# An edge loop on one core: a register load and score sums moved behind an aggregation, exponents ahead of one-hot rows, rectification one step earlier into six places

## The reference

```python
h_src = h[src]; h_dst = h[dst]                       # h: 6250 x 8 heads x 32
alpha = einsum(h_src, a_src) + einsum(h_dst, a_dst)
enc = relu(edge_attr @ edge_W.T + edge_b)            # 100000 x 8 x 32
alpha = alpha + sum(enc * h_dst, axis=-1)
alpha = where(alpha >= 0, alpha, 0.2 * alpha)
ex = exp(alpha - segment_max(alpha, dst)[dst])
out = segment_sum(h_src * ex / segment_sum(ex, dst)[dst], dst)
```

## Time and profile before

| | |
|---|---|
| median of three runs | 2097.55 us |
| the profiled execution | 2095.04 us, span 2093.2 us |
| mean granted TensorE clock | 0.968 |
| `edges`, first encoding to last sum | 102 to 1169 us |
| PE busy | 1919.5 us (92%) |
| DVE busy | 1517.0 us (72%) |
| ACT busy | 1290.6 us (62%) |
| POOL busy | 1206.5 us (58%) |

### The profile page before, as it was taken

One profiled execution on the slowest core, in us unless ns is written; L12 is line 12 of the kernel. 1 busy time (PEld: TensorE's weight loads), 2 busy tenths in 40 slices (PEclk: granted clock), 3 DMA queues, 4 the chain that ended last, 5 costly groups with the idle time before them and its releaser, 6 DMA issues. The chain is left out here.

```text
span 2093.2 us, 45236 instructions
## 1 busy us (share of the span) xinstructions
PE 1919.5 (92%) x12492; PEld 1499.5 (72%) x12492; DVE 1517.0 (72%) x3421; ACT 1290.6 (62%) x3667; POOL 1206.5 (58%) x1137
## 2 busy tenths in 40 slices
PE   7679999999999999999999486899999999999997
PEld 5446666666666666666666245899999999999996
DVE  8769899999999999999999878444444444444442
ACT  4458888888898888888898475233333333333332
POOL 3377777777777776766664000455555555555553
PEclk9879999999999999999999788999999999999998
DMA  9555555555555555555553895222222222222221
GB/s 253 163 153 151 150 157 153 155 153 158 155 155 150 154 151 147 146 144 145 145 141 91 282 331 80 54 36 39 39 36 36 38 40 37 36 36 39 39 37 23
DMA packets 161230, 242.12 MB, mean 116 GB/s; under 512 B 36895, under 2 KB 115519, under 8 KB 160866
## 3 DMA queue, kind: packets, MB, share of 16 engines
q0 software_dynamic: 61920, 139.45, 28.2%
q1 hardware_dynamic: 90362, 92.12, 15.0%
q10 hardware_dynamic: 8712, 7.65, 1.1%
HBM read 202.22 MB, written 36.91 MB: 114 GB/s over the span
## 5 line engine op out<-in xcount | busy, mean ns | idle before, releaser
L750 POOL DMA_INDIRECT arena<-h_tab,src x784 | 757.9, 967 | 285.7 <-issue 195.9
L1774 ACT ACTIVATE arena<-psum,arena 128x128 f32<-128x128 f32 x840 | 239.5, 368 | 519.6 <-PE psum L1724 519.6
L965 PE MATMUL psum<-arena 128*128 128x264 f32 x1760 | 475.3, 394 | 0.7 <-DVE arena L1062 0.6
L1724 PEld LDWEIGHTS psum<-arena 128*128 128x128 f32 x3360 | 393.8, 193 | 7.6 <-issue 2.4
L1724 PE MATMUL psum<-arena 128*128 128x128 f32 x3360 | 394.3, 276 | 2.0 <-DVE arena L1796 2.0
L1740 PE MATMUL psum<-arena 128*128 x1680 | 379.9, 380 | 0.0
L944 PE MATMUL psum<-arena 128*128 128x256 bf16 x2640 | 373.8, 277 | 5.0 <-DVE arena L1039 4.8
L965 PEld LDWEIGHTS psum<-arena 128*128 128x128 f32 x1760 | 300.3, 191 | 82.9 <-issue 46.8
L1686 POOL DMA_INDIRECT out_rows<-arena,src x105 | 212.8, 2027 | 247.6 <-DVE arena L1809 244.6
L1740 PEld LDWEIGHTS psum<-arena 128*128 128x128 f32 x1680 | 311.7, 191 | 37.4
L823 ACT ACTIVATE arena<-iota_row,nrel 128x128 f32<-128x128 f32 x880 | 301.7, 392 | 57.6 <-PE psum L965 57.5
(11 more groups left out here) (242 smaller groups left out, 1921.6 us busy)
## 6 DMA issues: line engine op xcount, KB each, us to landing
arena<-rel_list SPq DMA_DIRECT2D x110, 256.0 KB
arena<-h_tab,src POOLq DMA_INDIRECT x784
arena<-ea_slots SPq DMA_DIRECT2D x440, 27.0 KB
arena<-in_x SPq DMA_DIRECT2D x12, 896.0 KB, 12.6
arena<-in_W SPq DMA_DIRECT2D x16, 512.0 KB, 8.3
arena<-in_W SPq DMA_DIRECT2D x8, 1024.0 KB, 12.3
h_tab<-arena SPq DMA_DIRECT2D x6, 952.0 KB, 9.2
out_rows<-arena SPq DMA_DIRECT2D x5, 896.0 KB, 12.2
```

The lines of the kernel that those rows point to most:

```text
L750: pool.indirect_dma_start(rows[:, (p % RING * U + k) * TW:(p % RING * U + k + 1) * TW], None, d.h_tab[:, :], bass.IndirectOffsetOnAxis(ap= ...
L965: last = nc.tensor.matmul(ps[:, AGG + a % 2, 0:HS], oh[:, a % OH, k, :], msg[:, a % MSG, k, :], start=(k == 0), stop=(k == U - 1))
L1724: last = nc.tensor.matmul(ps[:, UP + 2 * b + h // 4, h % 4 * P:(h % 4 + 1) * P], w_now[:, b, m, h * P:(h + 1) * P], xT[:, b, m * P:(m + 1) ...
L1774: last = nc.scalar.activation(hT[:, b, h * P:(h + 1) * P], ps[:, UP + 2 * b + half, h % 4 * P:(h % 4 + 1) * P], ACT.Gelu, bias=b1_now[:, b ...
```

## The change

Two things are reordered on TensorE, four on ScalarE, and buffers are moved to make room.

TensorE: in step 1 of a chunk `aggregate` now stands ahead of `reduce`. In step 7 the load of eight registers stands behind `join` and `aggregate`, where it stood ahead of both.

ScalarE: `relu(g)` moves from step 2g to step 2g - 1, ahead of the same step's one-hot rows; a sixth place (`RENC` = 6) holds the encoding that is now made earlier. `exponent` moves ahead of `one_hot` in step 0. `clear_ahead` moves from odd steps to the even steps behind them.

Memory: the one-hot rows of the two sides trade regions, and half of the weights of expert 1 is loaded at the start of `attend` instead of the end of `edges`.

```diff
-RING, RENC, OH, OT, EB, MSG = 18, 5, 4, 3, 3, 4
+RING, RENC, OH, OT, EB, MSG = 18, 6, 4, 3, 3, 4
-W1_EARLY = (1, 2, 3, 4)
+W1_EARLY = (2, 3, 4)
...
-                if g >= 8 and g % 4 == 0:
+                if g >= 9 and g % 4 == 1:
                     act.wait_ge(back_done, g // 4 - 1)
...
-                if t < SLOTS and t % 2 == 0:
-                    relu(t // 2)
+                if t == 0:
+                    relu(0)
+                if t % 2 and t + 1 < SLOTS:
+                    relu((t + 1) // 2)
...
+                for ch in due(t, 8):
+                    exponent(ch)
                 if 0 <= a + 2 < SLOTS:
                     one_hot(a + 2)
...
                 for ch in due(t, 8):
-                    exponent(ch)
                     node_scale(ch)
+                if t % 2 == 0 and CS < t <= SLOTS + CS:
+                    if t == CS + 2:
+                        act.wait_ge(split, 4)
+                        nc.scalar.activation(acc[:, 0:HS], c.ones[:, 0:1].to_broadcast([P, HS]), ACT.Copy, scale=0.0).then_inc(cleared, 1)
+                    if t % CS == 2:
+                        act.wait_ge(hd_done, t - CS - 2)
+                    clear_ahead(j_first, (t - 2) % CS // 2)
...
                     expand(t, js)
-                    if t % CS == CS - 1 and t + 1 < SLOTS:
-                        js = load_words(nc, c.slots[0:1, t + 1:t + 1 + CS], mybir.EngineType.PE, 0, J - 1)
                 for ch in due(t, 4):
                     to_heads(ch)
                 for ch in due(t, 7):
                     join(ch)
+                if 0 <= a < SLOTS:
+                    aggregate(a)
                 for ch in due(t, 1):
                     reduce(ch)
-                if 0 <= a < SLOTS:
-                    aggregate(a)
+                if t % CS == CS - 1 and t + 1 < SLOTS:
+                    js = load_words(nc, c.slots[0:1, t + 1:t + 1 + CS], mybir.EngineType.PE, 0, J - 1)
...
-            for e in (0, 5, 6, 7):
+            for e in (0, 1, 5, 6, 7):
                 sp.dma_start(w1[:, 1, e, :], d.W1[e, P:2 * P, :]).then_inc(c.w1_loaded, 16)
```

More of the change, by code:

```diff
@@ L76 @@
 BIG = 1.5e38
-assert GROUPS * GT == J == FIRST[-1] and max(TILES) == GT and SLOTS % CS == 0 and RENC == CS // 2 + 1
+assert GROUPS * GT == J == FIRST[-1] and max(TILES) == GT and SLOTS % CS == 0 and RENC == CS // 2 + 2
 W1_AT = 0
@@ L695, in edges @@
         renc = take(RENC * 2 * 512).rearrange("p (b x e) -> p b x e", b=RENC, x=2)
-        oht = take(OT * 2 * UE).bitcast(BF16).rearrange("p (b e) -> p b e", b=OT)
         ea = c.ea
@@ L701, in edges @@
         alpha = take(P)
+        oh = take(OH * UE).rearrange("p (b k n) -> p b k n", b=OH, k=U)
         assert at <= W1_AT + (X + W1_EARLY[0]) * HID
         at, end = REST_AT + EA_WORDS, ARENA
-        oh = take(OH * UE).rearrange("p (b k n) -> p b k n", b=OH, k=U)
+        oht = take(OT * 2 * UE).bitcast(BF16).rearrange("p (b e) -> p b e", b=OT)
         leaky, fwd, top, ex = (take(P) for _ in range(4))
```

## The result

The change makes the kernel slower: 2133.51 us (median of 4 runs, 2132.05 to 2135.39) against 2099.22 us for the kernel before in the same comparison, a ratio of 1.0173 with a 95% interval of 1.016 to 1.0186. Forecast were 2099.5 us with a range of 2083 to 2110. The profiled execution of after took 2135.39 us, span 2133.6.

A forecast was written before the change was run, and what follows sets the result against it. Gathers were taken to bound the first half, a ring over nearly full PE, DVE and ACT the last 32 chunks. Parts 3.90 + 4.69 + 3.93 + 6.17 = 18.69 against 18.66 us, +1 us, plus 1 for weights: 2099.5 us, range 2083 to 2110.

The forecast's parts named there:

- Two regimes: Loop: gathers pace chunks at 19.26 us until 527.9 us; engine order can matter only in the last 32 chunks.
- Rival D: Whole loop: gathers pace it to the end, so ordering does nothing; 2097.5 us, chance within the forecast's 0.42.
- Exponent ahead of the one-hot rows: Step 0: exponent comes 0.69 us sooner, which takes away PE's whole 0.44 us wait.
- Aggregation ahead of `reduce`: Step 1 on PE: `reduce` no longer directly follows six matmuls paced by address arithmetic; gain 0.15 us, bounds 0 and 0.2.
- PE's register load behind the aggregation: Step 7: the load fits under the aggregation; steps 6 to 0 fall from 4.42 to 3.93 us.
- Rectification in the odd steps: Chains over PE and ACT: steps 2 to 4 grow 3.63 to 3.90 us, steps 4 to 6 grow 3.85 to 4.69.
- the term for `chain`: Steps 4 to 6: 0.33 us from the aggregation's end to the next encoding, within the 4.69 us chain.
- Rival A: ACT step 5: both loads run while `relu` waits, square 0.90 us behind it; 0.46 us a chunk, 2085 us, chance 0.19.
- Rival B: Chains over PE and ACT are smaller, 0.2 to 0.3 us a chunk; 2091 us, chance 0.17.
- VectorE gets the rest as waits: Whole chunk: VectorE's work is 18.12 us, so the remainder becomes waits, for `chain` in step 6.
- Rival C: Steps 4, 6 and 0: chains cost more than the rest returns; 0.35 us a chunk, 2110 us, chance 0.22.
- Weights of expert 1: `attend` and `route`: moving 524,288 bytes into this stage costs 0 to 1.5 us, taken as 1.

The follow-up runs named there:

- `relu_odd_only_3`: Kernel before with rectification in odd steps ahead of one-hot rows, six places, rest of loop order as before, on base C's constant waits: 2110.76 us, ratio 1.0072.
- `product_first`: base C with VectorE's product ahead of its message in step 0; on an occasion with the kernel before at 2530 us: 2504.1 us, ratio 0.988.
- base C: Changed kernel with ScalarE's and POOL's waits on loaded counts put on constants, dropping ScalarE's second load in step 5: 2111.94 us, ratio 1.0072; other occasions 2504.6, 2499.4.

## Why the prediction was wrong

**Two regimes, and where the first one ends.** That gathers pace the first chunks was right, but 527.9 us was only the end of a stretch that I had chosen. In the kernel before, ScalarE's last wait for landed rows is at 450.1 us, and a chunk takes (527.9 - 453.1) / 4 = 18.7 us from the 17th exponent on:

```profile
L866 ACT ACTIVATE arena<-arena x5: 303/303/304, 453.1 to 527.9; 128x128 f32<-128x128 f32 x5
```

So the 19.26 us were a mean over both regimes, and the order could matter in 38 chunks, not in 32. At 19.46 us the loop is slower than the gathers sooner still: ScalarE's last wait for rows is at 354.8 us, the exponents of chunks 10 and 11 are still 0.6 us ahead of the kernel before, and behind them nearly every chunk loses. From the 3rd exponent to the 21st a chunk takes 19.66 us, where I had said that it stays at 19.26:

```profile
L866 ACT ACTIVATE arena<-arena x19: 292/309/310, 179.6 to 533.5; 128x128 f32<-128x128 f32 x19
```

32 times +0.77 would have been 25 us, and it was 35. I had used the regime as a bound for gains and applied it to a loss. Rival D, that gathers pace the loop to the end, is out by the same rows.

**Exponent ahead of the one-hot rows.** PE's 0.44 us for it is gone, as forecast; `to_rows` starts 0.50 us behind its encoding. The profile after shows ACT waiting for VectorE's subtraction instead, 0.16 us. Right in itself; the time came back 0.17 us further, see below.

**Aggregation ahead of `reduce`, -0.15 us.** Wrong. From `to_rows` to the encoding of step 2 PE takes 735.63 - 729.18 = 6.45 us, where it took 721.38 - 715.48 = 5.90. The prediction looked at the product behind the `expand` of step 2 and not at the one that `expand` of step 1 waits for, two slots back, by the same semaphore. In the kernel before that product ended at 715.35 us and `expand` started at 715.65; without the 0.44 us that PE lost to the exponent it would have started at 715.21. It was on time only because PE was late. With PE early, VectorE is what step 1 waits for: 0.35 us of idle array, 0.48 us from start to start. That `expand` of step 2 now stands behind `reduce` closes the ring over VectorE's product; with `reduce` moved out of it the chunk is 0.16 us shorter (18.61 against 18.45 us), with one load more.

**PE's register load behind the aggregation, -0.5 us.** The idle 0.33 us ahead of `join` is gone and the part fell from 4.42 to 4.05 us. But the kernel with the load in its old place (`relu_odd_only_3`) has 4.05 us there too, so the fall can't be put down to the load. In that kernel PE's load starts 0.25 us ahead of the encoding of step 6 (median of 21 chunks), in the kernel before 0.80 us behind it. The encoding waits for a rectification there, a wait that the prediction put at 0. In step 6 the rectification ended at 710.06 and the encoding started at 710.20, 0.33 us behind `chain`, where it starts 0.15 us behind it in after (724.48 to 724.63); in step 0 the encoding's weight load waits for it too (between 700 and 1100 us):

```profile
PEld psum L928 <- ACT arena L816: 7.4, 21, 0.5
```

The sooner rectification takes this wait away, and with it, it seems, what exposed the load. Both kernels with 4.05 us have other changes around it (an aggregation that waits, or the load moved), so that isn't separated, and what the load's new place is worth by itself stays open.

**Rectification in the odd steps, +0.27 and +0.84 us.** Measured +0.30 and +0.68, with the chain as it was summed up: 0.43 us from encoding to rectification, 0.92 or 1.36 to the square, a waiting aggregation of 1.16 us. Too large was only the term for `chain`, 0.33 against 0.15 us, since it held the wait of the encoding just told. PE's matmuls wait for L827 once a chunk, in step 6, for 0.6 us; I had said twice. Rival A is out: the first of the two loads starts at 720.5 us, when the rectification that had waited starts (720.53), the square comes 1.36 us behind it, and taking one load away gave 0.45 us back.

```profile
L658 ACTq TENSOR_LOAD <-slots x2: 550/636/723, 720.5 to 721.1; - x2
```

The rule of the Trainium skill (Perfetto Trace Analysis, Per-engine timelines) that the sequencer decodes the next instruction while one waits does not hold for these loads in this trace. Rival B (smaller chains) is out as well.

**VectorE gets the rest as waits.** This is the step at which the sum broke. VectorE waits 0.81 us for `chain` in step 6, as I said it would, but I treated these waits as harmless, since VectorE's total of 18.12 us was below the chunk. It does its long maxima behind that wait and comes to step 0 late: from `chain`'s scan to the end of step 0's product it takes 4.95 us without a pause (724.74 to 729.69), and 4.94 in the kernel before (710.41 to 715.35). PE's part from step 0 to 2, which I summed for PE alone at 6.17 us, depends on that product and takes 6.95. Four parts, each the larger of two engines' needs, don't add up to a chunk when what ends one part late is what starts the next.

**Rival C** named the place that decided, VectorE behind a later `chain`, and the wrong victim (the exponent; it was the product), with half the price (0.35 against 0.78 us). It had 0.22 where it should have had most. With 0.3 us of room on VectorE and 1.1 us more of chains in front of it, a loss deserved more.

**Weights of expert 1.** 0 to 1.5 us were forecast. `attend` and `route` take 146.6 us in the one profile of before, 151.4 in that of after, and 147.1 to 148.4 in the seven other profiles with the late load at 2097 us, so 0.5 to 2 us. The 3 us more in after don't belong to the edit as far as these seven tell; they came once more among the profiles on other occasions (151.2 in `product_first`), and why stays open.

## What to carry over

Where a move ties two engines that only followed each other before (here ScalarE's one-hot rows to an encoding of the step just before), sum the ring through all engines, with each one's queue order, for a whole period; the largest of the parts, taken part by part, is too low. An instruction that may wait belongs behind the ones that somebody else waits for: the same rectification cost 16 us ahead of the one-hot rows and nothing behind them (base C). And before an order is changed, look at what stood ready only because its consumer was late.

## What the runs showed of the hardware

Of two loads of eight registers (550 and 723 ns) behind a rectification that waits, neither starts before it does; the first runs under it, and the second costs 0.45 us a chunk, 21.6 us in all here. Where ScalarE has work queued they cost the loop nothing: with the rectification behind the one-hot rows the part was 3.68 us with both loads as with one.

One occasion differs from another by more than the change makes. On five of twelve occasions the same kernel before took 2530 to 2550 us and not 2097, one of them on a chip that bears the number of one of the seven others, so that it need not be the chip. A profile there (base C) has granted clock 0.913 and these waits between 600 and 1100 us:

```profile
POOL arena L755 <- DVE arena L1056: 172.7, 73, 6.3
...
ACT arena L821 <- remote: 59.2, 16, 5.2
...
DVE arena L1046 <- remote: 43.7, 17, 4.4
ACT arena L850 <- remote: 37.8, 11, 5.5
```

Single stops of 4 to 6 us on one engine or another, which no semaphore of the program ends ("remote"). All of the extra time lies ahead of `attend`, which starts at 1570.7 us and not at 1185.2; from there on the two profiles of base C take 924.1 and 925.6 us. All variants with six places ran 0.6 to 1.6% faster than the kernel before there, the changed one's base too, while at 2097 us most of them, and the changed kernel, are slower than it. What stops the engines I can't tell from the trace; that a sixth place lets the loop ride over such stops is a guess.
